# Cross-attention in fp32: where the last two partial sums of exponentials are joined

## The reference

```python
xq  = _ada_ln(x_q,  t_vec, Wss_q,  bss_q)        # layer norm, then (1 + scale) * h + bias from silu(cond)
xkv = _ada_ln(x_kv, t_vec, Wss_kv, bss_kv)
q = (xq @ Wq + bq).reshape(B, Lq, 16, 32)
kv = (xkv @ Wkv + bkv).reshape(B, Lkv, 2, 16, 32)
scores = einsum('bqhd,bkhd->bhqk', q, kv[:, :, 0]) / sqrt(32)
out = einsum('bhqk,bkhd->bqhd', softmax(scores), kv[:, :, 1]).reshape(B, Lq, 512)
return x_q + (out @ Wp + bp)
```

## Time and profile before

| what | value |
|---|---|
| median of 3 runs | 2161.34 us (2161.32, 2161.34, 2163.28) |
| the profiled execution | 2162.3 us, its span 2160.6 us |
| PE busy | 2133.8 us, 99% of the span |
| DVE busy | 1911.3 us, 88% |
| ACT busy | 1815.4 us, 84% |
| PE's granted clock | 0.999 of full speed |

### The profile page before, as it was taken

The page is one execution under the profiler, slowest core; times in us unless marked ns, Lnnn a source line. Parts: engine busy times, 40 slices in busy tenths (PEclk is TensorE's granted clock), DMA queues, the critical chain, the costliest instruction groups (busy, mean ns, idle before and its releaser), DMA issues.

```text
span 2160.6 us, 56104 instructions
## 1 busy us (share of the span) xinstructions
PE 2133.8 (99%) x24986; PEld 611.9 (28%) x24986; DVE 1911.3 (88%) x1179; ACT 1815.4 (84%) x1940; POOL 17.3 (1%) x28
## 2 busy tenths in 40 slices
PE   7999999999999999999999999999999999999998
PEld 3444322222222222222222222222222222222222
DVE  2435799999999999999999999999999999999998
ACT  1212899999999999999999999999999999998995
POOL 0001000000000000000000000000000000000000
PEclk9999999999999999999999999999999999999999
DMA  8445522234232422234223332233233322242211
GB/s 295 148 156 179 161 84 61 77 88 121 70 82 70 139 70 77 61 103 110 82 70 99 110 82 70 77 96 108 70 82 90 100 75 77 70 116 83 77 54 51
DMA packets 189059, 210.23 MB, mean 97 GB/s; under 512 B 17286, under 2 KB 120462, under 8 KB 188812
## 3 DMA queue, kind: packets, MB, share of 16 engines
q1 hardware_dynamic: 187228, 206.06, 32.4%
q10 hardware_dynamic: 1584, 0.53, 0.1%
HBM read 169.33 MB, written 37.22 MB: 96 GB/s over the span
## 4 chain that ended last, share of the span: by engine, by line
PE 98%; DVE 1%; DMA 0%; issue 0%; ACT 0%; POOL 0%; SPq 0%; DVEq 0%
PE bank L1093 40%; PE bank L1105 37%; PE bank L1173 5%; PE bank L1122 4%; PE bank L1011 4%; PE bank L1022 4%; PE bank L1135 1%; PE bank L1148 1%; PE bank L1231 1%; PE bank L991 1%; DVE stats L1448 0%; PE bank L1158 0%; DVE arena L1462 0%; DMA arena<-in_ctx_dram 0%; POOL rstd L938 0%
## 5 line engine op out<-in xcount | busy, mean ns | idle before, releaser
L1344 ACT ACTIVATE arena<-bank,shift 128x1024 f32<-128x1024 f32 x1600 | 1691.0, 1113 | 139.5 <-PE bank L1093 137.8
L1656 DVE TENSOR_TENSOR arena<-arena 128x2048 f32<-128x2048 f32 x736 | 1655.7, 2288 | 98.8 <-ACT arena L1344 94.2
L1093 PE MATMUL bank<-qs,ks 32*64 32x512 f32 x12800 | 918.5, 613 | 1.1 <-ACT arena L1303 0.7
L1105 PE MATMUL bank<-arena,vg 128*32 128x512 f32 x6400 | 852.3, 605 | 1.2 <-ACT arena L1344 1.2
L1093 PEld LDWEIGHTS bank<-qs,ks 32*64 32x64 f32 x12800 | 205.3, 129 | 371.5 <-ACT arena L1344 221.8
L1105 PEld LDWEIGHTS bank<-arena,vg 128*32 128x32 f32 x6400 | 125.8, 108 | 650.5 <-ACT arena L1344 649.7
L1173 PE MATMUL bank<-wp,arena 128*32 128x168 f32 (+2 forms) x2464 | 153.6, 321 | 0.0
L1122 PE MATMUL bank<-xt,wq 128*32 128x256 f32 x1792 | 137.7, 379 | 0.0
L1173 PEld LDWEIGHTS bank<-wp,arena 128*32 128x32 f32 x2464 | 80.1, 110 | 184.3 <-issue 164.6
L1303 ACT ACTIVATE arena<-bank,bk_c 128x512 f32<-128x512 f32 (+1 forms) x28 | 18.0, 642 | 129.9 <-PE bank L1011 129.9
L1122 PEld LDWEIGHTS bank<-xt,wq 128*32 128x32 f32 x1792 | 58.2, 110 | 134.0 <-issue 118.2
(11 more groups left out here) (88 smaller groups left out, 424.1 us busy)
## 6 DMA issues: line engine op xcount, KB each, us to landing
ks<-k_full SPq DMA_DIRECT2D x160, 320.0 KB, 3.1
vg<-v_full SPq DMA_DIRECT2D x160, 320.0 KB, 3.9
p_b<-p_tails SPq DMA_DIRECT2D x128, 128.0 KB, 4.1
arena<-in_x_dram SPq DMA_DIRECT2D x13, 1024.0 KB, 7.9
q_full<-qs SPq DMA_DIRECT2D x32, 256.0 KB, 2.0
out_dram<-arena SPq DMA_DIRECT2D x32, 256.0 KB, 2.0
arena<-l_recip SPq DMA_DIRECT2D x28, 256.0 KB, 5.7
k_full<-arena SPq DMA_DIRECT2D x6, 1024.0 KB, 4.4
```

The source lines that it names most:

```text
L1093: mm = nc.tensor.matmul(bank[out, 2 * (i % RING) + h % 2, :], ks[rows_of(h), keys], qs[rows_of(h), g, :], start=True, stop=True)
L1105: mm = nc.tensor.matmul(bank[rows_of(h), o_bank(u), :], vg[:, t, rows_of(h)], pt[t % PR][:, h, :], start=(t == 0), stop=False, skip_group_ ...
L1344: nc.scalar.activation(pt[t % PR][:, 2 * pair:2 * pair + 2, :], bank[:, first:first + 2, :], ACT.Exp, scale=SCALE, bias=shift[:, g:g + 1]) ...
L1656: nc.vector.tensor_tensor(a[:, :, :], (pt[t - 1] if k <= 2 else a)[:, :, :], pt[t % PR][:, :, :], ALU.add).then_inc(p_added, 1)
```

## The change

`apart` is gone, and every unit is treated in the one way: DVE's add at L1666 is made in all 32 units, and PE takes the denominators from `acc` alone everywhere. `added(u)` becomes `ADDS * u` with ADDS = 24.

```diff
-            def apart(u):
-
-                return u % NG < NG - 1 and u // NG in (0, NB - 1)
-
             def added(u):
 
-                return sum(ADDS - apart(v) for v in range(u))
+                return ADDS * u
...
-                        sums = (acc[of % 2], odd[of % 2]) if apart(of) else (acc[of % 2],)
-                        for a in sums:
-                            for h in range(HG):
-                                mm = nc.tensor.matmul(bank[rows_of(h), side_bank(u), halves_of(half)], ones[:, :],
-                                                      a[:, h, halves_of(half)], start=(a is sums[0]), stop=(a is sums[-1]),
-                                                      skip_group_check=True)
+                        for h in range(HG):
+                            mm = nc.tensor.matmul(bank[rows_of(h), side_bank(u), halves_of(half)], ones[:, :],
+                                                  acc[of % 2][:, h, halves_of(half)], start=True, stop=True,
+                                                  skip_group_check=True)
...
-                        if not apart(u):
-                            dve.wait_ge(p_added, added(u) + ADDS - 1)
-                            nc.vector.tensor_tensor(sums[0][:, :, :], sums[0][:, :, :], sums[1][:, :, :], ALU.add
-                                                    ).then_inc(p_added, 1)
+                        dve.wait_ge(p_added, added(u) + ADDS - 1)
+                        nc.vector.tensor_tensor(sums[0][:, :, :], sums[0][:, :, :], sums[1][:, :, :], ALU.add
+                                                ).then_inc(p_added, 1)
```

## The result

| | kernel before | changed kernel |
|---|---|---|
| median | 2163.4 us (20 runs, 2160.39 to 2165.71) | 2158.91 us (20 runs, 2157.28 to 2161.84) |
| ratio, with its 95% interval | | 0.9983 [0.9976, 0.9990] |
| profiled execution: span | 2160.6 us | 2156.9 us |

The ratio is a saving of about 3.7 us (2.2 to 5.2). The forecast was 4.9 us, 2156.4 against a median of 2161.34 that three runs had given. The time falls into the range, but "faster by over 0.2%", which had most of the chance, did not come: the saving is 0.17%. A saving of 4.9 us is still inside the interval, so whole times alone don't say which term was wrong; the profiles do.

What follows compares the result with a forecast made beforehand. PE's steps were taken as the bound, with DVE counting at the end; -5.16 from PE plus 0.2 of DVE lag gave -4.96, rounded to -4.9, so 2156.4 us against the median 2161.34, range 2155.7 to 2159.3.

Steps and rivals of the forecast that it cites:

- faster by over 0.2%: Whole kernel: outcome class for a time below 2157.0 us, given a chance of 0.60.
- PE's term, 12 x 0.43 = 5.16 us: Units 1 to 3 and 29 to 31: 12 steps shrink from 2.90 to 2.47 us, saving 5.16 us.
- rival (c): PE's steps do not shrink, something else holds their length; time stays at 2161.3 us; chance 0.07.
- The first block's adds at nothing: Units 1 to 3: DVE's added adds fit its idle time, so none of their work reaches the path.
- 0.88 us of margin in unit 29: Unit 29, step 5: DVE's first add ends 0.88 us before ACT's exponentials need its slot, so ACT does not stop.
- The lag at the end, 0.2 us: Units 29 to 31: DVE's room falls 0.2 us short, which reaches the kernel's end; bounds 0 and 2.58 us.
- a room of 9.0: Units 29 to 31: waits and loose spacing let DVE take in 9.0 us, against a need of 9.18 us.
- my steps through the units: Adds stepped one by one: lags of 3.9, 2.3 and 2.5 us at units 29, 30, 31; 0.15 more at the last add.
- Rival (a): Last block keeps nothing, through more DVE lag or reciprocals 1 us later; only 2.58 us saved, 2158.8 us; chance 0.10.
- Rival (b): Only DVE's idle time is room; the last block saves 0.95 of 2.58 us, total 2157.8 us; chance 0.10.
- the prediction's own signs: Among them, ahead of the last denominators: PE's idle time growing well beyond 1.44 + 0.2 us would prove the forecast wrong.
- The line of 0.2%: Whole kernel: 0.2%, 4.3 us, is what measurement can tell from no change; the forecast lay just beyond it.

Runs made afterwards that it cites:

- all_divided: Sums left divided in units 0 to 30, compared with the changed kernel: 2185.31 us in one run, attention 26.27 us longer.
- last_only: Kernel before with the change in the last block alone (units 0 to 2 stay divided): ratio 0.9989 to the kernel before, attention 1.83 us less.
- second profile of the changed kernel: The changed kernel run again, nothing altered: ratio 0.9984 to the kernel before (11 runs), attention 1910.10 us.
- extra_u31: Changed kernel plus one unused 128x512 DVE add after step 12 of unit 31: attention 1909.88 us against 1909.13.
- early_inverse: Changed kernel with the inversion of block 6's denominators one step earlier in unit 28 (step 9, not 10): attention 1909.19 us against 1909.13.
- first_only: Kernel before with the change in the first block alone (units 28 to 30 stay divided): ratio 0.9991 to the kernel before, attention 2.42 us less.
- extra_u29: Changed kernel plus one unused 128x512 DVE add after step 12 of unit 29: attention 1911.07 us against 1909.13.

## Why the prediction was right and wrong

- **PE's term, 12 x 0.43 = 5.16 us: right.** Units 1 to 3 gave 0.83 us each, the units of the last block 0.86, together 5.03 to 5.07. The reading of the step lengths rather than of the busy share carried it; rival (c) is out.
- **The first block's adds at nothing: right**, and so in the middle blocks (all_divided). The 0.88 us of margin in unit 29 held too.
- **The lag at the end, 0.2 us: mis-sized, and this is the step that failed.** It measured 0.37 us in the better profile, 0.74 in last_only and 1.20 (9.00 less 7.80) in the second profile of the changed kernel. The mechanism, lateness of DVE that reaches the last add, was right. Two things in its size were wrong. First, the joining add was priced at 2.20 us where the rows show 2.32 for an add that waits for its forerunner, though I had used 2.32 for unit 29. With 2.32 the need is 3 x 2.32 + 2.58 = 9.54 against a room of 9.0, some 0.5 us short. That is what the runs have at the wait of 1.43 us from which I started: extra_u31, with 1.4 us, was 3.98, 2.59 and 2.82 us late at units 29, 30 and 31, where my steps through the units had 3.9, 2.3 and 2.5, and by the rule of the table 2.82 is a lag of 0.49. Second, the wait for the reciprocals was taken as a fixed 1.43 us. It is 1.0 to 2.6 us from one execution to the next. Before the change this had no effect on the end, with idle time left in unit 31 (7.80 in each profile without the new adds there, with waits of 1.4 to 1.8 us); after it, each microsecond above the floor is paid. The floor is a third thing that the sum of room against need does not show, since it treats three units as one account: room at the start of unit 30 can take in what came before it but not what unit 30 adds itself, so an early transfer brings the lag to 0.37 us and no lower (early_inverse). One of the prediction's own signs told of the miss: PE's idle time ahead of the last denominators is 1.80 and 2.64 us, above 1.44 + 0.2.
- **Rival (a)** had just this place and this cause ("the reciprocals come 1 us later"), with the whole 2.58 us as its price. It is the right mechanism at the wrong size: 0.4 to 1.2 us, since lateness adds to the end and does not undo PE's shorter steps. Rival (b)'s 0.95 us saved in the last block is refuted: 2.2 us in the first profile (2.58 - 0.37), 1.83 in last_only, and 1.4 in the second profile (2.58 - 1.20), where the late transfer accounts for the rest.
- **The base.** Two of the first three runs, and so their median of 2161.34, came from the lower of the two groups that twenty runs show. The forecast time leaned on it; the saving did not. That 2158.91 is next to the 2158.8 of rival (a) is a coincidence for the same reason: (a) took 2.58 us off the lower base. Of the 2.5 us between forecast and measured time 2.06 are the base.
- **The line of 0.2%.** With 5.0 us from PE and 0.4 to 1.2 from DVE, the attention's saving is 3.8 to 4.7 us, and of the changed kernel's two profiles one lies on each side of 4.3. A chance of 0.60 for "faster" rested on the 0.2. From the start of the attention to the end the two profiles saved 4.48 and 2.04 us against the one profile before; the 3.7 us of the whole runs lies between, and how each term makes it up over many runs is not shown.

The first stage lies at 228.1 to 231.8 us in these profiles, which is most of the scatter that one run shows. It goes with the clock: in six of the fourteen profiles PE's granted clock was at its lower level of 1.2 GHz, 0.5 of full, for a few microseconds from about 21 us on (0.79 in the mean from 20 to 28 us), and these six have 230.1 to 231.8 us, the other eight 228.1 to 229.9. The first transfer of the context took 3.8 to 6.2 us on the chain that ended last, without such an order. Neither was tried by a run.

## What to carry to other kernels

Work moved to an engine with idle time is free only as long as idle time remains *between it and the next place where that engine is waited for*; add the room up from behind, from the end of the kernel, unit by unit, and not over a block; and price the moved instruction by a row in which it waits for what it will wait for. Once that room is used up, the engine passes on every delay that it used to swallow, here a transfer that varies by 1.6 us, so price the spread of the waits ahead of it too and not only the one in the trace. The last instance of a repeated pattern has no cover: the best gain here was to leave out the joining add there alone.

## What was not expected of the hardware

In three profiles PE lost its full clock at the last denominators, after it had stood idle ahead of them: the granted clock was 0.5, the lower of the two levels (1.2 and 2.4 GHz), from 2141.0 to 2144.2 us in the second profile of the changed kernel, where it was still full at 2140.8 and PE stood idle until 2141.38, and from 2139.7 to 2142.9 in extra_u31. Windows of 8 us from the last denominators on (PE busy, granted clock), in the same order:

```profile
2141.38:2149.38 8.00, 8.00 (x27) 0.82 0.00 0
```

```profile
2138.87:2146.87 8.00, 8.00 (x27) 0.79 0.00 0
```

The first four of those products took 1.93 us in the one for 1.07 at the full clock, and from the denominators to the end there were 18.59 and 18.55 us, against 17.12. Idle times of 1.44 to 2.18 us never came with this in these profiles; 2.53, 2.64 and 2.80 did, and 3.27 (extra_u29) did not, so the length of the idle time alone does not decide, and no run sets it apart from other causes. It is 1.5 us in an execution where it happens, more than the lag of the last add in these three profiles, 1.1 to 1.4 us. The versions with unit 31 divided, with no idle time there, kept the full clock until the end in all three profiles.

Whether this is a reason why the changed kernel's runs gave less than its first profile is not shown, because the kernel before may lose the clock too. The mean granted clock of its runs is on record for 48: 0.998 in 23 and 0.999 in the others, and in its profile, the only one, it is 0.999. The changed kernel has 0.998 in 16 of 31 runs. The versions with unit 31 divided have it in none of 26, but first_only and last_only, where PE stands idle at the end as well, have it in only one of 20. The mean doesn't tell in which stretch the clock was lost.
